# Wide attention of an eight-block network: the subtraction of the softmax maxima in four partition quarters, for both query halves at once

## The chip, the core and the metric

The kernel runs on one core of a Trainium2 chip, as one launch. The metric is device time in microseconds of that core; what is compared is the median over runs. TensorE is called PE in the profile, VectorE DVE, ScalarE ACT, GpSimd POOL, and SyncE, which issues nearly all DMAs, SP.

## What is computed

Eight blocks follow one another on a batch of 4 sequences of 1024 tokens with 128 channels: four attentions and four feed-forward parts, each with a residual sum and a layer norm. The change touches only the seventh block, a wide attention with 16 heads of 64 channels. Cut to what matters:

```python
Q = (x @ Wq.T + bq).reshape(B, N, 16, 64)      # K and V alike
scores = einsum('bnhd,bmhd->bhnm', Q, K) * (SCALE * adaptive_scale)[None, :, None, None]
w = softmax(scores, axis=-1)
attn = einsum('bhnm,bmhd->bnhd', w, V).reshape(B, N, 1024)
y = x + (attn @ Wo.T + bo)
return (y - mean(y)) / sqrt(var(y) + 1e-5) * gamma + beta
```

## The kernel before, in words

`wide_attention` works through 32 units: 4 batches times 8 pairs of heads. Head `a` of a pair (0 or 1) lies on partitions 64a to 64a+63 of `q` and `k`. A unit u does the following.

- Projections, made two units ahead: `project_q`, `project_k`, `project_v`.
- 16 maximum tiles (`max`), made one unit ahead, for unit u+1: TensorE multiplies bf16 copies of 128 queries by 512 keys for both heads (L3290), VectorE reduces the two PSUM banks to their maxima (L3386). After the last one, `send` joins them (L3393), turns them by a transpose (L3297), splits each maximum into a high and a low bf16 part (L3398, L3400), and SP copies those into partition rows of `max_rows` (L3233), two rows per head, all 1024 queries wide.
- 16 score tiles (`score`), two for each of 8 blocks of 128 keys (`kb`), one for each half `h` of the queries. In a score tile TensorE first writes the negative maxima into the two banks, as a product of ones with `max_rows` over 64 rows per head (L3306, all rows but two are zero), and then adds the fp32 scores, also over 64 rows per head (L3309; an fp32 product is two instructions). The products of the two heads lie on different 64-row halves of the array and run side by side.
- ScalarE takes the exponential of the two banks (L3487). `weigh` multiplies the tiles of the key block before by V (L3323), fp32, over 128 rows and 64 columns per head, into two banks of their own. The sums over keys are added up beside it: half 0 on VectorE (`add`, L3205), half 1 on GpSimd (`add_beside`, the same line). `sums`, `invert` and `divide` (L3334, L3414, L3409) finish the unit before.

The order of everything is one list, `plan`, written out by loops over u and kb. Every engine walks through the whole list and issues its own share, so the order of the list is the order on each engine. `MAXIMA[kb]` says how many maximum tiles of the next unit go with a key block: in this kernel all of them stand between and right behind the two score tiles, ahead of `weigh`. `gate_work` puts in steps of a bisection for the next block's gates (215 small VectorE steps, two per key block), `next_later` the steps that end a batch: the output product, two norms, the transposes.

PSUM has 8 banks: two for `weigh`, and three slots of two banks that all the other steps take in turn. `with_banks` deals them out: a step takes the slot after the one that the step before took, and TensorE waits, ahead of the step's first instruction, until the step that held this slot three takings earlier has been read out (for `max` its reduction, counter `maxed`; for `score` its exponential, `exped`):

```python
for step in plan:
    if step[0] in released:
        at = (at + 1) % n
        out.append((step, at, done[at]))
        done[at] = released[step[0]](*step[1:])
```

## Time and profile before

| | us |
|---|---|
| median of 3 runs (lowest, highest) | 6142.39 (6139.86, 6145.15) |
| the profiled execution's own time | 6135.48 |
| its span | 6133.7 |
| PE busy, of the span | 5606.5 (91%) |
| DVE busy | 3945.9 (64%) |
| ACT busy | 2828.8 (46%) |
| POOL busy | 1087.6 (18%) |
| mean granted TensorE clock | 0.941 of full speed |

The wide attention's own matrix products run from 4053 to about 5600 us of the span. How to read the rows further down: a timeline row gives the start, the length, the engine and line, the output and the inputs; "x4" means that four instructions in a row were drawn into one, from the start of the first to the end of the last. A TensorE instruction's length holds its way through the array too, which overlaps with the next instruction; what a step costs TensorE is therefore read from its start to the start of the next step. "[0.32 <-DVE ...]" is idle time ahead of the row and what ended it.

### The profile page before, as it was taken

Reading aid. Unit: us, or ns where it says so; the run is one execution under the profiler, and the core shown is the slowest. Engines: PE = TensorE matmul, PEld = TensorE weight load, DVE = VectorE, ACT = ScalarE, POOL = GpSimd, SP = SyncE. Lnnn points to the kernel's source line nnn. Section 1 sums busy time; section 2 is a strip of 40 time slices with the busy share of each in tenths; the row PEclk is TensorE's granted clock in tenths of the full one; section 3 lists DMA queues with packets and bytes.
Section 4 is the critical chain, followed back from the end, with each engine's and each line's share of the span. In section 5 each row is a group of like instructions: output and inputs, shape, how many; then the busy total and the mean of one; then the engine's idle time right before and its main releaser. Section 6 shows DMA issues by size and latency. Waiting matters only on the chain. (4 is left out here: it accounts for less than half of the span.)

```text
span 6133.7 us, 88302 instructions
## 1 busy us (share of the span) xinstructions
PE 5606.5 (91%) x33238; PEld 2856.0 (47%) x33238; DVE 3945.9 (64%) x6471; ACT 2828.8 (46%) x4476; POOL 1087.6 (18%) x731
## 2 busy tenths in 40 slices
PE   7989998688989999989999899979999989997999
PEld 2333333345557777742222376633333433334776
DVE  6777775785577777769888512257777777774412
ACT  4656566322233333347767633434444444443333
POOL 0010000120022222320210000014333334332000
PEclk7989999788989999989999899989999999998999
DMA  3111110001111111111111100000000000001000
GB/s 89 39 30 28 30 26 13 0 0 21 34 37 25 30 27 30 27 22 30 34 35 26 36 1 1 1 19 15 12 12 15 8 13 13 12 12 39 4 4 8
DMA packets 119146, 131.41 MB, mean 21 GB/s; under 512 B 44580, under 2 KB 67924, under 8 KB 118404
## 3 DMA queue, kind: packets, MB, share of 16 engines
q1 hardware_dynamic: 118216, 125.07, 9.5%
q8 instruction: 263, 4.31, 0.3%
q14 instruction: 163, 1.34, 0.1%
q10 hardware_dynamic: 504, 0.69, 0.1%
HBM read 102.29 MB, written 22.07 MB: 20 GB/s over the span
## 5 line engine op out<-in xcount | busy, mean ns | idle before, releaser
L542 DVE TENSOR_REDUCE l_max_parts<-l_p 128x2 f32<-128x1024 f32 x512 | 602.9, 1220 | 207.8 <-PE l_p L518 170.8
L688 ACT ACTIVATE attn_w<-l_p 128x512 f32<-128x512 f32 x1024 | 554.1, 596 | 378.6 <-PE l_p L678 270.1
L3386 DVE TENSOR_REDUCE wide_max_parts<-wide_p 128x2 f32<-128x1024 f32 x512 | 614.6, 1220 | 166.0 <-PE wide_p L3290 153.5
L2345 PE MATMUL caus_p<-caus_x_one,big 128*128 128x129 f32 x4608 | 639.1, 286 | 13.0 <-ACT big L2420 13.0
L542 DVE TENSOR_REDUCE rot_max_parts<-rot_p 128x2 f32<-128x1024 f32 x512 | 601.8, 1219 | 68.8 <-PE rot_p L518 66.6
L2420 ACT ACTIVATE big<-caus_p 128x512 f32<-128x512 f32 (+3 forms) x768 | 345.8, 489 | 592.5 <-PE caus_p L2331 436.3
L2345 PEld LDWEIGHTS caus_p<-caus_x_one,big 128*128 128x128 f32 x4608 | 589.2, 198 | 50.0 <-ACT big L2420 14.3
L2776 ACT ACTIVATE moe_hidden<-moe_experts,moe_b 128x512 f32<-128x512 f32 x512 | 349.6, 687 | 509.2 <-PE moe_experts L2764 508.8
L3309 PE MATMUL wide_p<-wide_q,wide_k 64*128 64x512 f32 x2048 | 525.6, 592 | 0.0
L3487 ACT ACTIVATE attn_w<-wide_p 128x1024 f32<-128x1024 f32 x342 | 349.7, 1024 | 352.9 <-PE wide_p L3309 351.5
L2786 PEld LDWEIGHTS moe_experts<-big,moe_hidden 128*128 128x128 f32 x4096 | 481.1, 194 | 51.3 <-issue 50.3
L2764 PE MATMUL moe_experts<-x_chn,big 128*128 128x512 f32 x1024 | 471.7, 604 | 33.2 <-ACT moe_hidden L2776 27.2
L2786 PE MATMUL moe_experts<-big,moe_hidden 128*128 128x128 f32 x4096 | 483.1, 277 | 0.0
L3205 POOL TENSOR_TENSOR big<-big,attn_w 128x1024 f32<-128x1024 f32 x128 | 328.4, 2565 | 436.4 <-PE wide_p L3290 425.0
L670 PE MATMUL l_p<-l_q_stack,l_k_stack 98*128 98x512 bf16 x1024 | 362.9, 391 | 24.1 <-ACT attn_w L688 22.1
L542 DVE TENSOR_REDUCE caus_max_parts<-caus_p 128x2 f32<-128x1024 f32 (+3 forms) x384 | 362.9, 956 | 24.7 <-PE caus_p L518 15.9
L3323 PE MATMUL wide_p<-attn_w,wide_v_tok 128*64 128x512 f32 x1368 | 336.4, 613 | 0.0
L670 PE MATMUL rot_p<-pair_q_stack,pair_k_stack 98*128 98x512 bf16 x1024 | 319.2, 392 | 17.9 <-ACT big L688 13.2
L688 ACT ACTIVATE attn_w<-rot_p 128x512 f32<-128x512 f32 x512 | 275.5, 596 | 125.2 <-PE rot_p L670 125.0
L688 ACT ACTIVATE big<-rot_p 128x512 f32<-128x512 f32 x512 | 274.8, 599 | 77.1 <-PE rot_p L670 74.9
L2797 DVE SCALAR_TENSOR_TENSOR x_mid<-moe_experts,moe_gates,x_mid 128x128 f32<-128x128 f32 x256 | 72.1, 344 | 368.8 <-PE moe_experts L2786 368.8
L2456 POOL TENSOR_TENSOR attn_w<-attn_w,caus_part 128x256 f32<-128x256 f32 x256 | 185.5, 725 | 695.8 <-DVE caus_part L2399 695.8
(516 smaller groups left out, 8372.8 us busy)
## 6 DMA issues: line engine op xcount, KB each, us to landing
pair_q_stack<-q_parts SPq DMA_DIRECT2D x576, 32.0 KB
pair_k_stack<-k_parts SPq DMA_DIRECT2D x576, 32.0 KB
wide_inverse<-inverse_rows SPq DMA_DIRECT2D x64, 256.0 KB
l_q_stack<-q_parts SPq DMA_DIRECT2D x279, 32.0 KB
l_k_stack<-k_parts SPq DMA_DIRECT2D x279, 32.0 KB
big<-in_L_ffn_W SPq DMA_DIRECT2D x32, 256.0 KB, 5.3
q_parts<-pair_parts_q SPq DMA_DIRECT2D x8, 768.0 KB, 3.6
k_parts<-pair_parts_k SPq DMA_DIRECT2D x8, 768.0 KB, 3.7
```

What stands on the lines that cost most here:

```text
L542: self.nc.vector.tensor_reduce(self.max_parts[:, 2 * p:2 * p + 2, n, half], pair[:, :, 0:self.width(n, half)], AX.X, ALU.max).then_inc(*se ...
L670: mm = nc.tensor.matmul(bank, heads.k_stack[i][0:STACK, j, kb * P:(kb + 1) * P], heads.q_stack[i][0:STACK, j, half * BANK:(half + 1) * BAN ...
L688: self.nc.scalar.activation(self.exps[t % len(self.exps)], bank, ACT.Exp).then_inc(*self.exped.up())
L2345: mm = nc.tensor.matmul(outs[o % 2][:, nq % 2 * (C + 1):(nq % 2 + 1) * (C + 1)], exps[h % 2][:, kb, nq * P:(nq + 1) * P], x_one[b % 2][:, ...
L2420: nc.scalar.activation(exps[h % 2][:, kb, lo:BANK], bank[:, lo:BANK], ACT.Exp).then_inc(*exped.up())
L2764: self.nc.tensor.matmul(self.up_banks[o % 3], self.w1[:, e, c * P:(c + 1) * P], cols, start=True, stop=True).then_inc(*self.up_mm.up())
L2776: self.nc.scalar.activation(self.hidden[o % 8][:, :], self.up_banks[o % 3], self.func, bias=self.b1[:, e, c:c + 1]).then_inc(*self.acted.up())
L2786: mm = self.nc.tensor.matmul(banks4(bank)[:, i, :], self.hidden[(first + c) % 8][:, i * P:(i + 1) * P], self.w2[:, e, c, :], start=c == 0, ...
L3309: mm = nc.tensor.matmul(side[:, a, :], k[u % SLOTS][own[a], kb * P:(kb + 1) * P], q[u % SLOTS][own[a], cols], start=False, stop=True)
L3323: mm = nc.tensor.matmul(out[own[a], h, :], v_tok[u % SLOTS][:, kb, own[a]], exps[t % E_BUFS][:, a, :], start=kb == 0, stop=kb == NT - 1)
L3386: nc.vector.tensor_reduce(max_parts[:, :, n, h], side, AX.X, ALU.max).then_inc(*maxed.up())
L3487: nc.scalar.activation(exps[t % E_BUFS], side, ACT.Exp).then_inc(*exped.up())
```

## The change

`max_rows` shrinks to 512 columns, and its four quarters of 32 partitions hold the maxima of (head 0, half 0), (head 0, half 1), (head 1, half 0) and (head 1, half 1), two rows each. `send` on SP issues 8 copies of 512 values where it issued 4 of 1024. The score tile of half 0 waits for its own slot and for that of half 1, then issues four subtractions, one on each quarter of the rows, into the four banks of both slots; then its scores; the tile of half 1 has scores only. For this the two score tiles of a key block stand next to each other. The maximum tiles are dealt out anew (`MAXIMA`): half of a block's number, rounded down, after the scores, the others after `weigh` and `add`. `send` moves from the last key block to the one before.

```diff
--- before.py
+++ after.py
@@ -3066,7 +3066,8 @@
     v_tok = [st.sbuf(f"v_tok{i}", [P, NT, C]) for i in range(SLOTS)]
     q_bf, k_bf = st.sbuf("q_bf", [P, T], BF16), st.sbuf("k_bf", [P, T], BF16)
     ones_bf = st.sbuf("ones_bf", [P, P], BF16)
-    max_rows = [st.sbuf(f"max_rows{i}", [P, T], BF16) for i in range(2)]
+    max_rows = [st.sbuf(f"max_rows{i}", [P, BANK], BF16) for i in range(2)]
+    quarter = [slice(j * P // 4, (j + 1) * P // 4) for j in range(4)]
     E_BUFS = 6
     more_exps = st.sbuf("exps", [P, (E_BUFS - 4) * T])
     exps = [core.attn_w[:, i * T:(i + 1) * T] for i in range(4)]
@@ -3092,7 +3093,7 @@
     rows, norm, turn, entmax = Rows(st, 2), Norm(st), Turn(st), Entmax(st, NT)
     units = [(b, m) for b in range(nb) for m in range(PAIRS)]
     N_LOADS, TILES, ADDS, PRODUCTS = 12, HALF * NT, NT - 1, 12
-    MAXIMA = [3, 2, 3, 2, 2, 2, 2, 0]
+    MAXIMA = [3, 3, 3, 2, 3, 2, 0, 0]
     IN_TILE = 2
 
 
@@ -3126,16 +3127,21 @@
         return [("add_beside", *waiting.pop(0), step)] if waiting else []
 
     plan = project(0) + [("max", 0, t) for t in range(TILES)] + [("send", 0)] + project(1)
+    todo = []
+
+    def maxima(u, n):
+        out = []
+        for _ in range(n if todo else 0):
+            out.append(("max", u + 1, todo.pop(0)))
+            out += beside(out[-1])
+        return out
+
     for u in range(len(units)):
-        todo = list(range(TILES)) if u + 1 < len(units) else []
+        todo.extend(range(TILES) if u + 1 < len(units) else [])
         for kb in range(NT):
-            for h in range(HALF):
-                plan.append(("score", u, kb, h))
-                for _ in range((MAXIMA[kb] + h) // HALF if todo else 0):
-                    plan.append(("max", u + 1, todo.pop(0)))
-                    plan += beside(plan[-1])
+            plan += [("score", u, kb, h) for h in range(HALF)] + maxima(u, MAXIMA[kb] // HALF)
             plan += beside(None)
-            if kb == NT - 1 and u + 1 < len(units):
+            if kb == NT - 2 and u + 1 < len(units):
                 plan.append(("send", u + 1))
             if u + 2 < len(units):
                 if kb == NT - 1:
@@ -3147,6 +3153,7 @@
                     plan.append(("project_q", u + 2))
             elif u:
                 plan += [("weigh", u - 1, NT - 1), ("keep", u - 1)]
+            plan += maxima(u, MAXIMA[kb] - MAXIMA[kb] // HALF)
             plan += gate_work(IN_TILE)
             if u and kb == 1:
                 plan.append(("sums", u - 1))
@@ -3227,12 +3234,13 @@
                     sp.wait_ge(*lo_kept.at(u + 1))
                     if u > 1:
                         sp.wait_ge(*scored.at(TILES * (u - 1)))
-                    for a in range(2):
+                    n = NT // HALF
+                    for j in range(4):
                         for r, part in enumerate((max_hi, max_lo)):
-                            row = a * WIDE + r
+                            row = j * P // 4 + r
                             nc.sync.dma_start(
                                 max_rows[u % 2][row:row + 1, :].rearrange("o (n t) -> o n t", t=P),
-                                part[a * NT:(a + 1) * NT, :]).then_inc(*row_sent.up(16))
+                                part[j * n:(j + 1) * n, :]).then_inc(*row_sent.up(16))
                 elif kind == "sums":
                     u = args[0]
                     sp.wait_ge(*sums_kept.at(u + 1))
@@ -3261,7 +3269,7 @@
             new = Fresh()
             pe.wait_ge(*loaded.at(16 * N_LOADS))
             pe.wait_ge(*ones_set.at(1))
-            for (kind, *args), i, left in plan:
+            for n_step, ((kind, *args), i, left) in enumerate(plan):
                 side = None if i is None else slots[i]
                 if left and new(*left):
                     pe.wait_ge(*left[0].at(left[1]))
@@ -3298,13 +3306,20 @@
                                         core.ident[:, :]).then_inc(*max_turned.up())
                 elif kind == "score":
                     u, kb, h = args
-                    for sem, n in ((q_kept, u + 1), (k_kept, u + 1), (row_sent, 64 * (u + 1))):
+                    for sem, n in ((q_kept, u + 1), (k_kept, u + 1), (row_sent, 128 * (u + 1))):
                         if new(sem, n):
                             pe.wait_ge(*sem.at(n))
                     cols = slice(h * BANK, (h + 1) * BANK)
-                    for a in range(2):
-                        nc.tensor.matmul(side[:, a, :], ones_bf[own[a], :], max_rows[u % 2][own[a], cols],
-                                         start=True, stop=False)
+                    if h == 0:
+
+                        _, i_next, left_next = plan[n_step + 1]
+                        if left_next and new(*left_next):
+                            pe.wait_ge(*left_next[0].at(left_next[1]))
+                        for half, to in enumerate((side, slots[i_next])):
+                            for a in range(2):
+                                rows_of = quarter[HALF * a + half]
+                                nc.tensor.matmul(to[:, a, :], ones_bf[rows_of, :],
+                                                 max_rows[u % 2][rows_of, :], start=True, stop=False)
                     for a in range(2):
                         mm = nc.tensor.matmul(side[:, a, :], k[u % SLOTS][own[a], kb * P:(kb + 1) * P],
                                               q[u % SLOTS][own[a], cols], start=False, stop=True)
@@ -3394,7 +3409,7 @@
                                             AX.X, ALU.max, negate=True).then_inc(*joined.up())
                     v.wait_ge(*max_turned.at(u + 1))
                     if u:
-                        v.wait_ge(*row_sent.at(64 * u))
+                        v.wait_ge(*row_sent.at(128 * u))
                     nc.vector.tensor_copy(max_hi[:, :], side[0:2 * NT, 0, 0:P]).then_inc(*hi_kept.up())
                     v.wait_ge(*hi_kept.at(u + 1))
                     nc.vector.tensor_tensor(max_lo[:, :], side[0:2 * NT, 0, 0:P], max_hi[:, :],

```

How the rows of the engines move, in the same key block (kb = 2) of a unit in the middle. In the lists "x4" counts matrix products as written, of which an fp32 one is two instructions on the chip.

TensorE before: subtraction, scores, maximum, subtraction, scores, two maxima, weighing, the next block's subtraction.

```order
L3306 MATMUL wide_p<-wide_max_rows,wide_ones_bf 128x512 x2
L3309 MATMUL wide_p<-wide_q,wide_k 128x512 x2
L3290 MATMUL wide_p<-wide_k_bf,wide_q_bf 128x512 x2
L3306 MATMUL wide_p<-wide_max_rows,wide_ones_bf 128x512 x2
L3309 MATMUL wide_p<-wide_q,wide_k 128x512 x2
L3290 MATMUL wide_p<-wide_k_bf,wide_q_bf 128x512 x4
L3323 MATMUL wide_p<-attn_w,wide_v_tok 64x512 x4
L3306 MATMUL wide_p<-wide_max_rows,wide_ones_bf 128x512 x2
```

TensorE now (L3321 subtraction, L3324 scores, L3298 maxima, L3338 weighing):

```order
L3321 MATMUL wide_p<-wide_max_rows,wide_ones_bf 128x512 x4
L3324 MATMUL wide_p<-wide_q,wide_k 128x512 x4
L3298 MATMUL wide_p<-wide_k_bf,wide_q_bf 128x512 x2
L3338 MATMUL wide_p<-wide_exps,wide_v_tok 64x512 x4
L3298 MATMUL wide_p<-wide_k_bf,wide_q_bf 128x512 x4
L3321 MATMUL wide_p<-wide_max_rows,wide_ones_bf 128x512 x4
```

Two of the three maximum tiles now stand behind the weighing and directly ahead of the next block's subtractions. That step takes two of the three slots; they were last held by this block's first and second maximum tile (in kb = 1, where `sums` takes a slot too, by its second and third).

VectorE before, from the maxima of kb = 2 on: three reductions, then the sum.

```order
L3386 TENSOR_REDUCE wide_max_parts<-wide_p 128x2 x3
L3205 TENSOR_TENSOR big<-big,attn_w 128x1024
L3386 TENSOR_REDUCE wide_max_parts<-wide_p 128x2 x2
L3205 TENSOR_TENSOR big<-big,wide_exps 128x1024
L3414 RECIPROCAL wide_sum_rows<-wide_sum_rows 16x128
```

VectorE now, from the sum of kb = 2 on; the row "x3" holds the second and third reduction of kb = 2 and the first of kb = 3:

```order
L3212 TENSOR_TENSOR big<-big,attn_w 128x1024
L3401 TENSOR_REDUCE wide_max_parts<-wide_p 128x2 x3
L3212 TENSOR_TENSOR big<-big,wide_exps 128x1024
L3401 TENSOR_REDUCE wide_max_parts<-wide_p 128x2
L3429 RECIPROCAL wide_sum_rows<-wide_sum_rows 16x128
```

The sum of the block now stands ahead of the second reduction.

## Rows read from the trace of the kernel before

**Rows 1.** Windows of the wide stage: span, busy per engine, granted clock, DMA.
```profile
4127.50:4433.10 305.60, 305.29 (x1577) 111.76 (x1577) 222.26 (x211) 149.06 (x148) 122.22 (x49) 1.00 0.05 13
4491.20:4597.70 106.50, 91.64 (x456) 32.78 (x455) 83.85 (x114) 48.74 (x50) 37.49 (x14) 0.97 0.04 11
```

**Rows 2.** Windows, of L3495 (one copy per unit) alone: ScalarE busy (count), clock.
```profile
4127.50:4433.10 305.60, 7.14 (x8) 1.00 0.05 13
```

**Rows 3.** Timeline, TensorE: one key block, start us, length, then the instructions.
```profile
4273.39 0.39 PE L3306 MATMUL wide_p<-wide_max_rows,wide_ones_bf 64*128 64x512 bf16 x2
4273.62 1.02 PE L3309 MATMUL wide_p<-wide_q,wide_k 64*128 64x512 f32 x4
4274.48 0.38 PE L3290 MATMUL wide_p<-wide_k_bf,wide_q_bf 64*128 64x512 bf16 x2
4274.69 0.38 PE L3306 MATMUL wide_p<-wide_max_rows,wide_ones_bf 64*128 64x512 bf16 x2
...
4275.77 0.39 PE L3290 MATMUL wide_p<-wide_k_bf,wide_q_bf 64*128 64x512 bf16 x2
4276.09 1.94 PE L3323 MATMUL wide_p<-wide_exps,wide_v_tok 128*64 128x512 f32 x8
4277.96 0.39 PE L3306 MATMUL wide_p<-wide_max_rows,wide_ones_bf 64*128 64x512 bf16 x2
```

**Rows 4.** Timeline, TensorE: sums, projections and the end of a unit.
```profile
4262.85 1.06 PE L3334 MATMUL wide_p<-big,ones 128*32 128x512 f32 x8
...
4287.09 1.98 PE L3273 MATMUL wide_p<-x_chn,big 128*128 128x512 f32 x4
4289.01 0.39 PE L3306 MATMUL wide_p<-wide_max_rows,wide_ones_bf 64*128 64x512 bf16 x2
...
4291.29 0.27 PE L3297 MATMUL wide_p<-ident,wide_neg_max 128*16 128x128 f32 x1
4291.40 1.98 PE L3273 MATMUL wide_p<-x_chn,big 128*128 128x512 f32 x4
4293.21 1.95 PE L3279 MATMUL wide_p<-big,x_chn 128*128 128x128 f32 x16
...
4296.95 0.39 PE L3306 MATMUL wide_p<-wide_max_rows,wide_ones_bf 64*128 64x512 bf16 x2
```

**Rows 5.** Timeline, VectorE: a block's maxima, sum, quotient, the next block's maxima.
```profile
4274.90 2.53 DVE L3386 TENSOR_REDUCE wide_max_parts<-wide_p 128x2 f32<-128x1024 f32 x2
...
4283.04 1.22 DVE L3409 TENSOR_TENSOR wide_att<-wide_att,wide_inverse 128x1024 f32<-128x1024 f32 x1
4284.18 2.38 DVE L3386 TENSOR_REDUCE wide_max_parts<-wide_p 128x2 f32<-128x1024 f32 x2
4286.48 1.22 DVE L3205 TENSOR_TENSOR big<-big,wide_exps 128x1024 f32<-128x1024 f32 x1
...
4290.96 0.18 DVE L3393 TENSOR_REDUCE wide_neg_max<-wide_max_parts 128x16 f32<-128x32 f32 x1
```

**Rows 6.** Timeline: VectorE's maxima, and the weight load that waited for the first.
```profile
4254.81 3.66 DVE L3386 TENSOR_REDUCE wide_max_parts<-wide_p 128x2 f32<-128x1024 f32 x3 [0.91 <-PE wide_p L3290]
...
4256.09 0.10 PEld L3290 LDWEIGHTS wide_p<-wide_k_bf,wide_q_bf 64*128 64x128 bf16 x2 [0.32 <-DVE wide_max_parts L3386]
```

**Rows 7.** Timeline, TensorE, layer 0: 32-row matrix products, then 128-row ones.
```profile
202.93 0.60 PE L518 MATMUL l_p<-l_k_stack,l_q_stack 32*128 32x512 bf16 x4
203.47 0.34 PE L526 MATMUL l_p<-l_near_max,flip_bf 128*128 128x192 bf16 x2
```

**Rows 8.** Timeline, TensorE: a wait of the wide stage, and the scores that came after.
```profile
4560.82 0.39 PE L3290 MATMUL wide_p<-wide_k_bf,wide_q_bf 64*128 64x512 bf16 x2 [3.60 <-ACT wide_exps L3487]
...
4564.24 1.67 PE L3309 MATMUL wide_p<-wide_q,wide_k 64*128 64x512 f32 x4
```

**Rows 9.** Timeline: a small step of the gates' bisection; a copy of maxima rows.
```profile
4800.14 0.22 DVE L2981 SCALAR_TENSOR_TENSOR wide_ent_power<-wide_ent_diff 128x64 f32<-128x64 f32 x1
...
4250.05 0.64 SPq L3233 DMA_DIRECT2D wide_max_rows<-wide_max_hi  x1
```


## The prediction

> **What bounds the kernel now.** I read the windows of the wide stage first. In the seven units from 4127.5 to 4433.1 us TensorE is busy 305.29 of 305.60 us at a granted clock of 1.00, VectorE 222, ScalarE 149 [rows 1]. The copy that ends a unit occurs 8 times there, so seven units take 305.60 / 7 = 43.66 us each [rows 2]. The batch's end is different: two units take 106.50 us, with TensorE busy 91.64 [rows 1]; VectorE does the norms there. The timeline of TensorE then gives the price of each step, start to start [rows 3]: a pair of subtractions 0.23, a score tile 0.86, a maximum tile 0.21 (0.32 where the weighing follows: 0.10 for the change from 64-row to 64-column products), a weighing 1.87, of which about 0.15 is the change of shape at both its ends. A key block with two maximum tiles takes 4277.96 - 4273.39 = 4.57 us and holds no gap. So removing TensorE work could pay; but only where nobody else has to finish first.
>
> **Why the order matters.** VectorE starts on a maximum tile 0.42 us after TensorE starts it (4274.48 to 4274.90 [rows 3, 5]), needs 1.22, and TensorE goes on 0.06 later (4254.81 + 1.22 = 4256.03, weight load at 4256.09 [rows 6]). From the start of a maximum tile to the reuse of its slot it is therefore 1.70 us at best. In the kernel before, the 1.87 us of weighing lie over this, since all maxima stand ahead of it. Steps that queue on VectorE follow each other every 1.15 us (4284.18 to 4286.48 for two reductions, 1.14 for the quotient ahead of them [rows 5]).
>
> **The change, part by part**
>
> *Subtractions.* Eight times a unit one pair of 0.22 goes. If four 32-row products run side by side, as the two 64-row ones do, the four cost 0.23. No row has four at once; the nearest are layer 0's 32-row pairs, four products in 0.54 us with 0.11 of it for the change of shape [rows 7], so two at a time. The Trainium skill (TensorE: Matmul & The Clock Gate, Measured speedup vs the span model) gives 3.07 times for four 32-row tiles instead of 4; by that the four would take 0.07 us more, an estimate that adds 14 us to the sum. No row here shows it.
>
> *Changes of shape.* Every block now goes from 32-row to 64-row products, and, where maxima stand behind the weighing, from 64-row to 32-row. Every change of shape in the rows costs TensorE: 0.10 into the weighing [rows 3], 0.11 in layer 0 [rows 7], and into full fp32 weights more: four projection products take 1.92 us instead of 4 x 0.43 = 1.72, with 0.43 for half a score tile [rows 3, 4], 0.10 at the end and 0.10 after the first of them. Bounds for 32-row to 64-row fp32 scores: nothing, and 0.30. I take 0.20, nearest to the projections, and 0.10 for the way back. The Trainium skill (TensorEngine Tiling (Array Packing), Key Properties) says that changing the tiling mode drains TensorE, and a change of tile alone does not; the rows agree for the changes that they hold, and that rule speaks against this edit. With no cost for the two new changes the sum would be 38 us less.
>
> *The wait.* This is the largest term. The four subtractions need both slots of their key block. With three maximum tiles (kb = 0, 1, 2, 4) the second slot is that of the first maximum tile behind the weighing. I count from the start of the subtractions: scores 0.43 to 2.15, first maximum 2.15, weighing 2.47, second maximum 4.34, third 4.55, next subtractions possible at 4.87. VectorE: first reduction at 2.57, sum 3.72, second reduction 4.87 to 6.09, so TensorE goes on at 6.14. ScalarE, busy less than half of the time [rows 1], takes each tile's exponential as soon as its scores stand and is not the last.
>
> The blocks of a unit, in us:
> - kb 0: no sum in between, second reduction at 4.76: 6.04.
> - kb 1: `sums` takes a slot as well (about 1.00 [rows 4]), so the subtractions wait for the third reduction too, 6.02 to 7.24: 7.29.
> - kb 2 and 4: 6.14 each.
> - kb 3 and 5: one maximum behind the weighing, its slot isn't needed: the second maximum at 4.34, its own 0.23 and a change of shape: 4.67 each.
> - kb 6: `send` now has to wait for VectorE: after kb 5 come its second reduction, the quotient (to 7.24, which is 2.57 into kb 6) and the joining of 0.18 [rows 5]; the transposes go at about 2.8 instead of 2.25. Then transposes and change 0.2, weighing 1.87, projection 1.92: 6.75.
> - kb 7: 0.43 + 1.72 + 0.12, projections 1.81 + 1.88, weighing 1.87 (4291.40 to 4296.95 in one [rows 4]): 7.83.
>
> The sum is 49.53 us against 43.66: **5.9 us more per unit**.
>
> *The stage.* 32 units, of which the last has no maxima (4.12 against 4.13 a block: nothing). Six units lie at the ends of batches. There TensorE already waits (106.50 - 2 x 43.66) / 2 = 9.6 us a unit, mostly because VectorE holds norms [rows 1], and the new waits fall partly into these; worked through block by block, one of them comes out 1.1 us longer. I take 1.2, with 0 and 5.9 as ends. The other 25: 25 x 5.88 = 147. With the gates' steps, two of 0.22 per key block [rows 9], VectorE reaches kb 4's reductions and kb 6's joining some 0.3 and 0.4 later, 0.7 in each of 12 units: 8. Batch ends: 7. `send` issues 8 copies instead of 4, each 0.64 of SP's time [rows 9]; they have a key block more to land in, and only at the stage's start nothing covers them: 3. GpSimd's sums start earlier in the list or as early. The smaller `max_rows` and its shorter clearing cost nothing, hidden behind the projections. Sum: 147 + 8 + 7 + 3 = 165. The profiled execution took 6135.5, which gives 6300; on the median, which is 6.9 higher, 6142.4 + 165 = **6307 us**.
>
> **Rivals**
>
> *Faster: the subtractions never wait.* Place: the start of a key block's four subtractions. If VectorE handed back the slots within 0.53 us of the second maximum (4.34 to 4.87), TensorE's work alone would count. With changes of shape at my price a unit would be 43.9 us, so nothing is won: 6142 + 7 = 6149. With free changes it would be 41.7, 2.0 x 31 less: 6080. Against it: the 0.42 + 1.22 + 0.06 of rows 3, 5 and 6 exceed 0.53 by 1.17 with VectorE idle, and VectorE isn't idle.
>
> *The four do not run together*, the change does not do what it says: two pairs in turn, 0.22 more in each of 8 blocks. In the waiting blocks it moves the first maximum and all behind it, so nothing hides it: 1.7 x 25 = 43 us more, 6350. For it: no row has four row tiles.
>
> *The clock drops.* A wait of 1.3 us in every second block could cost TensorE its 2.4 GHz. After the wait of 3.60 us the scores took 1.67 instead of 1.02 [rows 8], at 1.2 GHz; with the subtractions ahead of them that is some 0.8 us. After 100 waits it would be 80 us: 6390. Against it: the window with 9.6 us of waits per unit, this long one among them, still stands at 0.97 [rows 1].
>
> *VectorE's queue costs more at batch ends* than I took: 6 x 4.7 = 28 us more, 6335. That lies in the range.
>
> **How the numbers follow.** My forecast (the wait at its price, changes of shape anywhere between their bounds, any batch end) has 0.78; two pairs in turn 0.08; the clock 0.04; no waits with paid changes 0.03; no waits and free changes 0.05; the remaining 0.02 are slower for reasons I don't see. The range: free changes 6307 - 38 = 6269, less 7 for batch ends that cost nothing, 6262; above, changes at 0.30 and 0.20, about 1.0 a unit or 25, and the batch ends at their upper end, 6360, which takes in the two pairs. About 0.2% (12 us) is what a measurement of this kernel tells from no change. Faster: 0.05. Within it: 0.03. Slower: 0.92.
>
> **What would show it.** In the profile after, TensorE's share in the middle units should fall from 99.9% to about 90%, with the clock at 1.00, and the list of waits should gain some 100 waits of the subtractions' weight load for VectorE's maxima, longest in kb 1, about 1.2 us each in view. The blocks should take about 6.0, 7.3, 6.1, 4.7, 6.1, 4.7, 6.8 and 7.8 us. The four subtractions should start within some 0.01 us of each other, and the first scores 0.4 after them. I would be wrong if a unit took under 44 us, if the subtractions waited for the exponential or the copies of the maxima instead, or if kb 3 and 5 grew as much as the others.

## The result, and the profile after

| | before | after |
|---|---|---|
| median, us (lowest, highest) | 6143.1 (6139.9, 6145.2) | 6359.3 (6357.3, 6364.0) |
| the profiled execution | 6135.5 | 6359.2 |
| its span | 6133.7 | 6357.5 |

Runs of both kernels taken side by side give a ratio of 1.0354, 95% interval 1.0336 to 1.0371: slower by 216 us, where 165 were forecast. The direction and the wait for VectorE came as forecast. The size is short by 51 us, and the time stands within 1 us of the range's upper end of 6360, so that the ratio's interval, put on the forecast's base of 6142.4, reaches from 6349 to 6370 and past it.

The page after, section 1 and the clock line of section 2:

```profile
PE 5653.0 (89%) x33238; PEld 2838.4 (45%) x33238; DVE 3978.2 (63%) x6471; ACT 2803.9 (44%) x4476; POOL 1061.9 (17%) x731
...
PEclk7989998879899999899999999899999999998999
```

TensorE's busy time has grown by only 46 of the 224 us by which the span grew (5606.5 to 5653.0), with the number of its matrix products the same; the rest is waiting. Windows of the middle units and of four units with the gates' steps (columns as in [rows 1]):

```profile
4134.80:4490.40 355.60, 308.94 (x1577) 105.70 (x1575) 233.71 (x210) 142.89 (x148) 115.04 (x50) 1.00 0.04 12
4725.20:4943.30 218.10, 186.44 (x902) 62.89 (x900) 146.27 (x184) 82.10 (x85) 70.37 (x29) 0.95 0.04 11
```

Seven units take 355.60 us, 50.8 each, against 43.66 [rows 1, 2]; TensorE is busy for 87% of them at the full clock. The second window, 54.5 a unit, was not foreseen: before, such a unit took 43.8 (from one copy of L3495 to the next), and now the granted clock is 0.95.

A block after, TensorE's timeline (start, length, instructions, idle time ahead and what ended it):

```profile
4302.32 0.40 PE L3321 MATMUL wide_p<-wide_max_rows,wide_ones_bf 32*128 32x512 bf16 x4 [1.27 <-DVE wide_max_parts L3401]
4302.65 1.99 PE L3324 MATMUL wide_p<-wide_q,wide_k 64*128 64x512 f32 x8
4304.47 0.38 PE L3298 MATMUL wide_p<-wide_k_bf,wide_q_bf 64*128 64x512 bf16 x2
4304.79 1.94 PE L3338 MATMUL wide_p<-attn_w,wide_v_tok 128*64 128x512 f32 x8
4306.66 0.39 PE L3298 MATMUL wide_p<-wide_k_bf,wide_q_bf 64*128 64x512 bf16 x2
4306.98 0.39 PE L3321 MATMUL wide_p<-wide_max_rows,wide_ones_bf 32*128 32x512 bf16 x4
```

The four subtractions start within 0.01 us of each other (in the trace at 4302.325, .331, .335 and .338) and end within 0.03: they do run at once. From them to the first scores there are 0.33 us (forecast 0.43), and from there to the maximum tile 1.82 (1.72): 2.15 for what took 2 x 0.22 + 2 x 0.86 = 2.16 in two parts [rows 3]. So the pair of products that is saved is paid back by the change of shape into the scores, as costed; the way back costs another 0.11 (maximum tile to subtractions 0.32, before 0.21).

The block itself is kb 3, with one maximum behind the weighing, and no wait stands at its end; its own start waited 1.27 us for the reduction, behind kb 2's two maxima. Over the whole stage, the idle time ahead of the subtractions (us in total, times):

```profile
  DVE wide_max_parts L3401: 412.4, 248
...
  ACT attn_w L3502: 4.3, 6
...
  DMA wide_max_rows<-wide_max_lo: 0.9, 1
```

(248 counts weight loads and products: 124 waits, at the start of kb 1, 2, 3 and 5 of each of 31 units.) The exponential and the copies of the maxima took next to no part: 8.1 and 0.9 us against 412.4. The blocks of a middle unit, start of the subtractions to the next start:

| kb | 0 | 1 | 2 | 3 | 4 | 5 | 6 | 7 | unit |
|---|---|---|---|---|---|---|---|---|---|
| forecast | 6.04 | 7.29 | 6.14 | 4.67 | 6.14 | 4.67 | 6.75 | 7.83 | 49.53 |
| measured | 6.13 | 7.34 | 6.21 | 4.65 | 6.20 | 4.65 | 7.81 | 7.81 | 50.80 |

Seven blocks are right to 0.1 us; kb 6 is 1.06 too short. The timelines of VectorE, GpSimd and TensorE at its start:

```profile
4318.03 1.22 DVE L3401 TENSOR_REDUCE wide_max_parts<-wide_p 128x2 f32<-128x1024 f32 x1
4319.16 2.26 DVE L3424 TENSOR_TENSOR wide_att<-wide_att,wide_inverse 128x1024 f32<-128x1024 f32 x1
4321.34 0.17 DVE L3408 TENSOR_REDUCE wide_neg_max<-wide_max_parts 128x16 f32<-128x32 f32 x1
...
4317.99 2.35 POOL L3212 TENSOR_TENSOR big<-big,attn_w 128x1024 f32<-128x1024 f32 x1 [3.87 <-PE wide_p L3298]
...
4321.66 0.27 PE L3305 MATMUL wide_p<-ident,wide_neg_max 128*16 128x128 f32 x1 [1.51 <-DVE wide_neg_max L3408]
```

The quotient, 1.22 us long before [rows 5], takes 2.26. GpSimd's sum ends at 4320.34 (4317.99 + 2.35), the quotient 1.08 later: it seems to have done its work after GpSimd was done. TensorE's transposes of the maxima wait for all of this. The reduction ahead of it, beside the same sum but reading PSUM, kept its 1.22. The same two engines in the kernel before:

```profile
4281.91 1.22 DVE L3205 TENSOR_TENSOR big<-big,attn_w 128x1024 f32<-128x1024 f32 x1
4283.04 1.22 DVE L3409 TENSOR_TENSOR wide_att<-wide_att,wide_inverse 128x1024 f32<-128x1024 f32 x1
...
4279.51 2.36 POOL L3205 TENSOR_TENSOR big<-big,attn_w 128x1024 f32<-128x1024 f32 x1 [2.21 <-PE wide_p L3290]
4284.08 2.40 POOL L3205 TENSOR_TENSOR big<-big,attn_w 128x1024 f32<-128x1024 f32 x1 [2.21 <-PE wide_p L3290]
```

There one of GpSimd's sums ends at 4281.87 and the next starts at 4284.08, so they stand around the two operations of VectorE but for the last 0.18 us of the quotient. The Trainium skill (SBUF — State Buffer, Who interferes with whom) says that a VectorE instruction with two inputs in SBUF contends with a GpSimd instruction that reads SBUF, over a pair of ports that it calls an exclusive lock, and that on trn2 a `tensor_reduce` never contends. Both halves of this agree with the rows: 2.26 us for the quotient beside the sum, 1.22 for the reduction beside it.

The gates' steps are small VectorE operations, many with both inputs in SBUF. One of them after, and under it before (count, then min/median/max in ns):

```profile
L3028 DVE COPY_PREDICATED wide_ent_low<-wide_ent_keep,wide_ent_mid x25: 161/1177/1214, 4746.3 to 5421.8; 128x8 f32<-128x8 uint32 x25
```

```profile
L3028 DVE COPY_PREDICATED wide_ent_low<-wide_ent_keep,wide_ent_mid x25: 163/165/2339, 4659.5 to 5230.7; 128x8 f32<-128x8 uint32 x25
```

What was 0.17 us in the median is now 1.18. Of all the gates' steps 28 took over 0.6 us, where 3 did before. One of the 28 on VectorE, GpSimd's sum beside it, and TensorE behind them:

```profile
4746.30 1.21 DVE L3028 COPY_PREDICATED wide_ent_low<-wide_ent_keep,wide_ent_mid 128x8 f32<-128x8 uint32 x1
...
4745.13 2.35 POOL L3212 TENSOR_TENSOR big<-big,attn_w 128x1024 f32<-128x1024 f32 x1 [3.86 <-PE wide_p L3298]
...
4752.05 0.61 PE L3321 MATMUL wide_p<-wide_max_rows,wide_ones_bf 32*128 32x512 bf16 x4 [2.13 <-DVE wide_max_parts L3401]
4752.59 3.42 PE L3324 MATMUL wide_p<-wide_q,wide_k 64*128 64x512 f32 x8
```

The small step ends with GpSimd's sum, 4747.51 and 4747.48. It holds the reductions behind it, so the subtractions wait 2.13 us instead of 1.27, and the clock falls: the same eight score products take 3.42 instead of 1.99, at 1.2 GHz. In the seven middle units, with waits of up to 1.5 us in five blocks of eight, the granted clock stayed at 1.00. The length of a wait alone does not tell: in the kernel before, the scores behind a wait of 2.76 us still ran at 2.4 GHz, 1.03 for the 1.02 of [rows 3].

```profile
5549.99 0.39 PE L3306 MATMUL wide_p<-wide_max_rows,wide_ones_bf 64*128 64x512 bf16 x2 [2.76 <-DMA wide_max_rows<-wide_max_lo]
5550.21 1.03 PE L3309 MATMUL wide_p<-wide_q,wide_k 64*128 64x512 f32 x4
```

### The profile page after: what moved, and what is told of

Its sections match the earlier page's. It is cut to its first block and busy times, and to the rows that moved or that the text cites. A ratio compares the mean times of both kernels' runs of the same rounds, so it can differ in the third digit from the quotient of the medians.

```text
span 6357.5 us, 88681 instructions
## 1 busy us (share of the span) xinstructions
PE 5653.0 (89%) x33238; PEld 2838.4 (45%) x33238; DVE 3978.2 (63%) x6471; ACT 2803.9 (44%) x4476; POOL 1061.9 (17%) x731
## 5 line engine op out<-in xcount | busy, mean ns | idle before, releaser
L3502 ACT ACTIVATE attn_w<-wide_p 128x1024 f32<-128x1024 f32 x342 | 332.8, 1021 | 493.5 <-PE wide_p L3324 493.4
L3324 PE MATMUL wide_p<-wide_q,wide_k 64*128 64x512 f32 x2048 | 534.3, 642 | 0.0
L3212 POOL TENSOR_TENSOR big<-big,attn_w 128x1024 f32<-128x1024 f32 x128 | 312.3, 2440 | 644.8 <-PE wide_p L3298 600.8
L3338 PE MATMUL wide_p<-attn_w,wide_v_tok 128*64 128x512 f32 x1368 | 338.3, 616 | 0.0
```

Source lines behind the costliest of these rows:

```text
L3324: mm = nc.tensor.matmul(side[:, a, :], k[u % SLOTS][own[a], kb * P:(kb + 1) * P], q[u % SLOTS][own[a], cols], start=False, stop=True)
L3338: mm = nc.tensor.matmul(out[own[a], h, :], v_tok[u % SLOTS][:, kb, own[a]], exps[t % E_BUFS][:, a, :], start=kb == 0, stop=kb == NT - 1)
L3502: nc.scalar.activation(exps[t % E_BUFS], side, ACT.Exp).then_inc(*exped.up())
```

## The experiments

Runs of the kernel before on the same chips gave medians of 6137 to 6142 us throughout. A time given without a ratio is that of a single execution.

**Which wait, and what lies over it.** Edit to the changed kernel: the larger half of a block's maxima ahead of the weighing.

```
-            plan += [...] + maxima(u, MAXIMA[kb] // HALF)
+            plan += [...] + maxima(u, MAXIMA[kb] - MAXIMA[kb] // HALF)
...
-            plan += maxima(u, MAXIMA[kb] - MAXIMA[kb] // HALF)
+            plan += maxima(u, MAXIMA[kb] // HALF)
```

> The changed kernel with the larger part of a block's maxima ahead of the weighing (two ahead, one behind, instead of one and two). Theory A (the subtractions wait for a slot whose reduction nothing covers): in blocks 0, 2 and 4 both slots were reduced under the weighing, the wait of 1.2 us in each goes; block 1 keeps its 7.3 us because the sums take a slot and the last maximum tile holds the other. A unit of the middle takes about 47.4 us instead of 50.8, the kernel about 6270. Theory B (the four 32-row subtractions and their changes of shape cost the time): the same instructions run, so about 6359 as the changed kernel.

Measured: 6294.7 us, ratio 1.0252 (1.0236 to 1.0267), a middle unit 47.6. The waits behind kb 0, 2 and 4 are gone (5.09 us a block), as expected. That behind kb 1, which has `sums` (1.18 us), and that of the transposes (1.51) stayed, and most units with gates took 50.6. So 65 of the 216 us go by one maximum moved in each of four blocks; the expected total, 6270, is 25 too low.

**All maxima ahead of the weighing.** Edit: `maxima(u, MAXIMA[kb])` ahead, the second call gone.

> The changed kernel with all maxima of a block ahead of the weighing. Theory A: no wait of the subtractions for VectorE's maxima in blocks 0 to 5; in its place the third maximum tile waits some 0.8 us for the exponential of the second score tile (slots), and the second 0.2 for that of the first. Blocks about 5.7, 6.7, 5.7, 4.7, 5.7, 4.7, 6.8, 7.8: 48 us a unit instead of 50.8, the kernel about 6270. Theory B: about 6359.

Measured: 6356.3 us, ratio 1.0348 (1.0332 to 1.0363). Blocks 0 to 5 came as expected (5.68 in kb 0, 2 and 4, 6.68 in kb 1, 4.77 with two maxima), but block 6 took 10.45, and 8.80 in the first two units, where the clock stayed up. VectorE, GpSimd and TensorE at its start:

```profile
4318.92 3.37 DVE L3423 TENSOR_TENSOR wide_att<-wide_att,wide_inverse 128x1024 f32<-128x1024 f32 x1
...
4315.56 5.65 POOL L3211 TENSOR_TENSOR big<-big,attn_w 128x1024 f32<-128x1024 f32 x2 [3.33 <-PE wide_p L3297]
...
4322.53 0.27 PE L3304 MATMUL wide_p<-ident,wide_neg_max 128*16 128x128 f32 x1 [2.50 <-DVE wide_neg_max L3407]
4322.73 3.51 PE L3337 MATMUL wide_p<-attn_w,wide_v_tok 128*64 128x512 f32 x8
```

Two sums of GpSimd now hold the quotient for 3.37 us, the transposes wait 2.50, and the weighing behind them runs at 1.2 GHz. What the waits gave back, GpSimd and the clock took. That made a third theory, tested with the next two.

**GpSimd's sums cut short.** Most of the sum over keys for query half 1 is left out. Edit to the changed kernel:

```
+        part = slice(0, BANK if h == 0 or kb == 1 else 16)
+        calls.tensor_tensor(to[:, :, part], first[:, :, part], exps[t % E_BUFS][:, :, part], ALU.add)...
```

> The changed kernel, with GpSimd's sums over all key blocks but the first cut to 16 of 512 columns of each head (the sum of query half 1 is left out for the others). Theory C (VectorE's operations with two inputs in SBUF wait until GpSimd's sum of 2.35 us has ended, which now starts just ahead of them): the quotient in block 5 takes 1.22 instead of 2.26 us, block 6 falls from 7.8 to 6.7, a unit of the middle from 50.8 to 49.7; where the gates' steps run, their steps of 1.2 us go back to 0.2, a unit falls from 53.7 and 55.4 to about 50.5, and the falls of TensorE's clock there go: about 6280 in all. Rival (these steps wait for something else, such as the copies of the inverses): 6359.

Measured: 6280.5 us, 79 less than the changed kernel. A middle unit 49.8, one with gates 50.1, as expected, and none of the gates' steps took over 0.6 us; the quotient is back:

```profile
4317.35 1.21 DVE L3426 TENSOR_TENSOR wide_att<-wide_att,wide_inverse 128x1024 f32<-128x1024 f32 x1
4318.48 0.18 DVE L3410 TENSOR_REDUCE wide_neg_max<-wide_max_parts 128x16 f32<-128x32 f32 x1
```

The clock stood at 0.99 between 4500 and 5500 us, where it was 0.96 in the changed kernel. Of the 79 us, 11 come from the six units at the batch ends. The kernel before with the same cut was not run; four of its quotients at the batch ends took 3.1 to 3.4 us, so it would probably gain too. The same cut with all maxima ahead:

> All maxima ahead of the weighing, and GpSimd's sums of all key blocks but the first cut to 16 of 512 columns of each head (left out for the others). The kernel with all maxima ahead missed its 6270 us only in block 6, where the quotient of 3.4 us and so the send waited. Theory C (VectorE's quotient waits until two sums of GpSimd have ended): block 6 falls from 10.5 to 6.8 us, a unit of the middle from 51.4 to 48.0, the kernel to about 6250. Rival (block 6 waits for something else that this order made late, the inverses or the exponentials): 6340 or more.

Measured: 6226.4 us, 130 below the uncut one, a unit 47.7, block 6 down from 10.45 to 6.65.

**Order or quarters?** The changed kernel's order of steps with the subtractions of before (64-row pairs, each ahead of its own score tile). `max_rows` is 1024 columns wide again, with four copies:

```
-                    if h == 0:
...
-                                rows_of = quarter[HALF * a + half]
...
+                    for a in range(2):
+                        nc.tensor.matmul(side[:, a, :], ones_bf[own[a], :], max_rows[u % 2][own[a], cols],
+                                         start=True, stop=False)
```

> The changed kernel's order with the subtractions of the kernel before (a pair of 64-row products at each score tile, each tile waiting for its own slot). Theory A: the first tile's 1.1 us of work now lie over the reduction of the second slot, so most of the wait goes: blocks with three maxima about 5.1, block 1 about 6.2, block 6 keeps its wait for the quotient; 46 us a unit, the kernel 6215 to 6245. Theory B: all of the loss goes, 6143 to 6160.

Measured: 6216.3 us, ratio 1.0120 (1.0103 to 1.0137), a unit 46.3: of the 216 us, 143 come with the subtractions, 73 with the order. The second half's subtraction comes 0.2 to 0.3 us late where the four together wait 1.27, since a score tile lies ahead of it.

The reverse, the old order and `send` in kb 7, with each tile's pair on 32 rows and eight copies:

```
+                    for a in range(2):
+                        rows_of = quarter[HALF * a + h]
+                        nc.tensor.matmul(side[:, a, :], ones_bf[rows_of, :], max_rows[u % 2][rows_of, :],
+                                         start=True, stop=False)
```

> The order of the kernel before, with the maxima in quarters and each tile's pair of subtractions over 32 rows instead of 64. It prices the change of shape alone: per block two ways from 32-row to 64-row fp32 scores at 0.20 and one more way from 64-row to 32-row at 0.10, 0.5 us, 4 us a unit. Priced so, the kernel takes about 6265. If such changes cost nothing, 6143.

Measured: 6276.4 us, ratio 1.0216 (1.0200 to 1.0231), a unit 48.6. TensorE's timeline:

```profile
4304.06 0.39 PE L3309 MATMUL wide_p<-wide_max_rows,wide_ones_bf 32*128 32x512 bf16 x2
4304.38 1.13 PE L3312 MATMUL wide_p<-wide_q,wide_k 64*128 64x512 f32 x4
4305.34 0.38 PE L3292 MATMUL wide_p<-wide_k_bf,wide_q_bf 64*128 64x512 bf16 x2
4305.65 0.39 PE L3309 MATMUL wide_p<-wide_max_rows,wide_ones_bf 32*128 32x512 bf16 x2
```

Against the steps of [rows 3], every step shown has grown by 0.10: subtraction to scores 0.32 (0.22), scores 0.96 (0.86), maximum tile to subtraction 0.31 (0.21). That is the price of a change of shape, with no wait in it: 0.49 a block in kb 3 to 6 (5.06 us instead of 4.57), as the 0.5 of my expectation, and about 3.5 a unit, since 0.2 of it in kb 0 and 2 falls where TensorE waited before. The other 1.5 us of the unit are a wait for the eight copies, which `send` in kb 7 issues too late:

```profile
4277.34 0.39 PE L3309 MATMUL wide_p<-wide_max_rows,wide_ones_bf 32*128 32x512 bf16 x2 [1.46 <-DMA wide_max_rows<-wide_max_lo]
```

Paid once a block, where the changed kernel has it, the change of shape eats the pair that is saved.

The last of this group keeps the changed kernel's order and its wait for both slots, but puts four 64-row products there:

```
-                                rows_of = quarter[HALF * a + half]
-                                nc.tensor.matmul(to[:, a, :], ones_bf[rows_of, :],
-                                                 max_rows[u % 2][rows_of, :], start=True, stop=False)
+                                nc.tensor.matmul(to[:, a, :], ones_bf[own[a], :],
+                                                 max_rows[u % 2][own[a], half * BANK:(half + 1) * BANK],
+                                                 start=True, stop=False)
```

> The changed kernel with its order and its wait for both slots, but with the subtractions of both tiles over 64 rows (two pairs in turn, 0.43 us) instead of four quarters. Theory A: the scores begin as late as with the quarters (0.43 + nothing against 0.23 + 0.20), so the blocks with three maxima keep their 6.1 to 6.2 us, block 1 its 7.3 and block 6 its 7.8; only the way back to 32 rows goes: about 6340 to 6355. Theory B (the quarters and their changes of shape make the loss): near the 6216 of the order alone.

Measured: 6359.9 us, a unit 50.8, both as the changed kernel. Subtractions and scores take 2.14 us there, 2.15 in the changed kernel. The quarters are worth nothing; the loss is the wait for two slots at once, in this order:

```profile
4306.13 0.61 PE L3318 MATMUL wide_p<-wide_max_rows,wide_ones_bf 64*128 64x512 bf16 x4 [1.27 <-DVE wide_max_parts L3399]
```

**Where `send` stands.** The changed kernel with `send` back in kb 7 (`NT - 2` to `NT - 1`):

> The changed kernel with the maxima sent in the last key block, as in the kernel before. Block 6 loses its wait for the quotient (1.7 us). Theory D: eight copies of 0.65 us on the queue plus their landing end some 2.5 us behind the next unit's first subtractions, which now wait for them; a unit takes about 51.6. If the copies' number does not matter, a unit takes 49.2 and the kernel some 45 us less than the changed one.

Measured: 6339.7 us, a unit 50.7. Block 6 shrank to 6.03, but eight copies in turn on SP's queue came too late for the next unit:

```profile
4337.45 0.40 PE L3321 MATMUL wide_p<-wide_max_rows,wide_ones_bf 32*128 32x512 bf16 x4 [1.48 <-DMA wide_max_rows<-wide_max_lo]
```

The wait exists, at 1.5 us and not the 2.5 of my expectation. Eight copies with `send` in kb 7 cost the same 1.5 us in the old order, above. In the order-only kernel, with four copies, the same edit is another matter:

> The order-only kernel with send back in the last key block; nothing is left out. Theory A: send's place in block 6, right behind VectorE's last maxima and the quotient, is what costs 1.8 us a unit there; in block 7, with four row copies as in the kernel before, nothing waits for it. Then a unit takes 44.5 us (0.9 left: second halves' subtractions waiting for a maximum's slot), and the kernel 6216 - 25 x 1.8 = 6171 us, still slower than before by 0.5%. Theory B: the copies then come too late for the next unit's first subtractions, as with send moved late in the changed kernel (1.5 us there, with eight copies); four copies should end 2.4 us sooner, so at most 0.2 us is expected of that. Above 6205 would speak for B.

Measured: 6152.6 us, ratio 1.0019 (1.0009 to 1.0028), a middle unit 44.5 as expected, and the total 18 below the forecast. So of the 76 us by which the order-only kernel is slower than the kernel before in this comparison (73 above), 64 are `send`'s place, one block ahead of its time, and 13 all else. The 18 came from the batch ends, which had not been in the sum: their six units took 50.4 to 53.1 us where the order-only kernel takes 51.9 to 58.0 and the kernel before 53.1 to 59.4. And GpSimd's part of the wait for `send`, in the order-only kernel:

> The order-only kernel with GpSimd's sums cut to 16 of 512 columns of each head (that part of the softmax sums is left out). In the order-only kernel a unit takes 46.3 us, 2.6 over the kernel before: about 1.8 at the transposes of the maxima (send), 0.9 at the second halves' subtractions. Theory A: of the 1.8, about 1.0 is the quotient held back by GpSimd's sum, as in the changed kernel. Then a unit should take 45.2 to 45.3 us, a unit with the gates' steps not over 45.6 (now 47.6), and the kernel about 6216 - 25 x 1.0 - 12 x 1.0 = 6180 us or a little less. Theory B: the wait of the transposes comes from the place of send alone, one block earlier; then units stay at 46.3 and the kernel above 6200.

Measured: 6145.5 us, a unit 45.3, one with gates 45.6: 1.0 of the 1.8 us of this wait, as theory A has it. The total fell 35 more than expected; the batch ends (49.2 to 53.4) gained from it too.

**Two tries at a faster kernel.** The kernel before with the weighings in pairs, behind every second block, the maxima dealt 3, 2, 3, 2, 3, 2, 1, 0, and `send` at the end of kb 6; nothing is left out:

> The kernel before with the weighings of two key blocks in a row, behind every second block (maxima 3, 2, 3, 2, 3, 2, 1, 0, sent at the end of block 6). If every change of shape costs TensorE what the runs show (0.10 into the weighing, 0.05 in it, 0.10 out of it), four of them less take 1.0 us from a unit: 42.6 instead of 43.6, the kernel about 6112. If the blocks without a weighing let TensorE wait for slots instead, it takes 6143 or more.

Measured: 6369.8 us, ratio 1.0378 (1.0361 to 1.0395). A miss: a middle unit took 48.3 us or more. With no weighing between, the maximum tiles follow too closely and wait for their slots, 2.4 us a unit, and the transposes of the maxima wait for VectorE, 2.2 a unit. One of the first kind:

```profile
4298.27 0.39 PE L3292 MATMUL wide_p<-wide_k_bf,wide_q_bf 64*128 64x512 bf16 x2 [1.60 <-DVE wide_max_parts L3388]
```

The other takes from the runs what was better: the changed kernel's order of maxima, in the two units after each batch alone.

```
+        norms = u > PAIRS and u % PAIRS in (1, 2)
...
+            if norms:
+                maxima(MAXIMA_NORMS[kb] // HALF)
...
+            if norms:
+                maxima(MAXIMA_NORMS[kb] - MAXIMA_NORMS[kb] // HALF)
```

> The kernel before, with the changed kernel's order of maxima in the two units after each batch alone (six of 32), where VectorE does the norms. In the order-only kernel with a late send these units took 50.5, 51.8, 53.1, 53.0, 50.4 and 51.3 us against 53.1, 53.3, 58.1, 59.4, 54.8 and 54.5 in the kernel before, 23 us less together; everywhere else the old order is better by 0.9 to 2.2 us a unit. Theory A: the gain belongs to these units' own order. Then this kernel takes about 6140 - 23 = 6117 us. Theory B: the gain is what was lost in the units around (work put off from there, the sum over four periods falls by 1, 7 and 4 us only); then at most 12 us are won, 6128 to 6140.

Measured: 6114.9 us against 6138.2, ratio 0.9959 (0.9945 to 0.9972): faster than both kernels, and 2 us from theory A's 6117. By the traces the six units give 16 us and the three before them 2. The window of the first two, to set beside the second of [rows 1]:

```profile
4490.40:4593.30 102.90, 93.10 (x459) 32.96 (x460) 82.56 (x115) 48.70 (x50) 37.35 (x15) 0.97 0.04 12
```

102.90 us for two units against 106.50. Two rows of the list of waits of this window, and under them the same of the kernel before (us in total, times, longest):

```profile
PEld wide_p L3301 <- ACT attn_w L3498: 4.9, 3, 3.4
PEld wide_p L3301 <- ACT wide_exps L3498: 3.4, 1, 3.4
```

```profile
PEld wide_p L3290 <- ACT attn_w L3487: 8.7, 9, 3.4
PEld wide_p L3290 <- ACT wide_exps L3487: 7.1, 5, 4.4
```

The weight loads of maximum tiles waited 15.8 us there for a slot that ScalarE's exponential had to free; with the other order it is 8.3. In the kernel before ScalarE was late because it waited for VectorE's norms, as this row of its timeline shows, ahead of the exponential that TensorE awaits at 4560.82 [rows 8]:

```profile
4558.13 0.30 ACT L171 ACTIVATE wide_std<-wide_mv,eps 128x8 f32<-128x8 f32 x1 [3.52 <-DVE wide_mv L155]
```

The order that costs time in the middle of a batch saves it here, where the engine that is late is another; that this is all of the gain is not shown.

## Why the direction came as forecast, and which step of the sum failed

**The wait** was the right term. The slots' count (0.42 + 1.22 + 0.06 from a maximum tile to the reuse of its slot) gave the blocks 0 to 5 and 7 within 0.1 us, told which of them would not wait, and named the release by VectorE. The run with both slots and no quarters shows that the wait, with what it brings on at the gates, carries the whole of what the subtractions cost, 143 us.

**The changes of shape**, taken at 0.20 + 0.10 where the bounds were 0 and 0.30 + 0.20, measured 0.20 + 0.10. The Trainium skill (TensorEngine Tiling (Array Packing), Key Properties) says that a change of tiling mode drains TensorE; the 0.10 us at each change between 32 and 64 rows agree with that. **The four at once** ran as four, and the rival of two pairs in turn falls: from four to the scores behind them it is 0.33 us, from two in the quarters-only kernel 0.32. The Trainium skill (TensorE: Matmul & The Clock Gate, Measured speedup vs the span model) has 3.07 times for four such tiles; these rows show no such loss.

**GpSimd's sums** are the step of the prediction that failed: "GpSimd's sums start earlier in the list or as early", costed at nothing. What counts is not when a sum starts but which operation of VectorE it runs beside. In the middle units before, its 2.4 us lay beside reductions that read PSUM. Now the maximum behind the weighing releases it, and it lies over the quotient, or, in the 14 units with gates, over the gates' step ahead of the quotient: 7.81 instead of 6.75 for block 6, about 27 us over 25 units. My sum took the quotient's 1.14 us from a row in which GpSimd stood still.

**The gates' steps**, costed at 8 us as plain length, suffer in the same way. By the distances between the copies of L3510, the eight full units with gates grew by 9.9 or 11.6 us each instead of 7.15, two more by 10, and the first units behind the batch ends by 12.9, 13.4 and 7.7: 47 us over the plain growth, where 8 were taken. The longer waits also brought **the clock** down: between the stage's first and last matrix product 26 stretches at 1.2 GHz began, against 9 before and 6 with GpSimd's sums cut. The rival priced this after each of 100 ordinary waits. In the middle units these never did it; most falls came behind the waits that GpSimd had lengthened, a few at the batch ends (4564, 4632, 5544 us) behind ordinary ones of 1.4. The blocks say what the clock costs. In the eight full units with gates, kb 5 takes 6.30 us instead of 4.65, with a fall at its start each time; kb 6 takes 9.85 in the four where a second fall comes and 8.20 in the four where none does, both behind a wait of 1.90. So a fall costs 1.65 us, and the twelve falls some 20 of the 29 us by which these eight units are over the plain growth (an estimate from these block times); VectorE's longer steps themselves are the rest, 7.07 instead of 6.20 in kb 4 and 8.20 instead of 7.81 in kb 6. Cutting the sums takes back 79 us: the quotient's part, most of the gates' part, and 11 at the batch ends.

**Batch ends**, taken at +7 with a note of VectorE's norms, gave 2 us back. Four quotients there took 3.1 to 3.4 us in the kernel before and 1.2 to 2.3 in the changed one, so GpSimd's overlap with them shrank; what this gave was not measured by itself. **The start** (3 us for eight copies) is about right: the first subtractions came 2.8 us later. By the profiled executions, 224 us apart: 25 x 7.15 = 179, 8 less in the last two of these, 47 at the gates, 2 less at the batch ends, 7 in the first two units with the start, together 223. On the medians, 216, the forecast of 165 misses 51. That this miss still ends at the range's upper end is luck: the 53 us of room there were made of dearer changes of shape and of batch ends, and neither came.

No run separates the clock from VectorE's longer steps in the 47 us at the gates; the share above is read from block times. Nor was a kernel tried with quarters, everything ahead of the weighing and GpSimd's sums moved away whole: with them cut short its unit is 47.7, so it could not have won.

## What to carry to other kernels

Before one step is made to need two buffers, look at what work lies between their last use and that step: here 1.87 us of weighing had covered 1.70 us of evacuation, and moving maxima behind it cost far more than the product saved. When VectorE operations with both inputs in SBUF are moved, set their times beside GpSimd's in the timeline, for a small step of 0.2 us can cost 1.2 there. And a merged matrix product that changes TensorE's tile shape has to save more than 0.3 us.

## What the runs showed of the hardware

Four 32-row products of 512 columns started within 0.01 us of each other and took 0.33 us to the scores behind them, where two took 0.32. A change between 32-row and 64-row products costs 0.10 us at the change and about 0.10 more in the fp32 products behind it. A quotient of VectorE took 1.22 us alone, 2.26 beside one sum of GpSimd and 3.37 beside two; a gates' step of 0.17 us took 1.21 there. Waits of 1.2 to 1.5 us in five of eight blocks left TensorE at 2.4 GHz. In the eight full units with gates it ran at 1.2 GHz for a stretch behind each wait of 2.13 us and behind half of the waits of 1.90 that followed, and such a stretch cost 1.65 us.
